# The prologue of a decoder kernel: statistics of all batch elements taken as their tokens land, and transposes placed between keys and values

## The reference

```
x = x + attention(layernorm(x))        # 16 heads of 8, causal, with a relative key term
x = x + cross_attention(layernorm(x), ctx)   # 77 context rows per element, heads normed again
x = x + experts(layernorm(x))          # 8 experts, the best 2 of them, and a shared one
```

## Time and profile before

| | us |
|---|---|
| median of 3 runs | 491.29 (489.8 to 491.65) |
| the profiled execution | 488.51 |
| its span, first to last instruction | 486.7 |
| PE busy in the span | 440.3 (90%) |
| DVE, ACT, POOL busy | 333.7, 265.6, 162.1 |
| first transpose of the prologue on PE | starts at 12.42 |
| first scores of the attention on PE | start at 36.96 |

### The profile page before, as it was taken

The page is one execution under the profiler, slowest core; times in us unless marked ns, Lnnn a source line. Parts: engine busy times, 40 slices in busy tenths (PEclk is TensorE's granted clock), DMA queues, the critical chain, the costliest instruction groups (busy, mean ns, idle before and its releaser), DMA issues.

```text
span 486.7 us, 17235 instructions
## 1 busy us (share of the span) xinstructions
PE 440.3 (90%) x7304; PEld 276.1 (57%) x7304; DVE 333.7 (69%) x668; ACT 265.6 (55%) x811; POOL 162.1 (33%) x95
## 2 busy tenths in 40 slices
PE   0778999999999799999799999998888989999996
PEld 0444655665755555655575675574445435666765
DVE  5555787666977667886847987867677596565633
ACT  2545646666466456555535655545544456554653
POOL 7148384332350963350851432093300000001000
PEclk9999999999999899999889999999989899999999
DMA  8221000000000000000000000000000004404150
GB/s 286 70 73 48 20 9 23 26 18 9 27 25 1 24 18 11 25 24 2 24 4 24 2 5 1 3 4 2 1 1 1 1 1 174 175 23 162 35 195 24
DMA packets 17465, 19.49 MB, mean 40 GB/s; under 512 B 1659, under 2 KB 14575, under 8 KB 17263
## 3 DMA queue, kind: packets, MB, share of 16 engines
q1 hardware_dynamic: 17391, 18.41, 11.2%
HBM read 16.17 MB, written 2.16 MB: 38 GB/s over the span
## 4 chain that ended last, share of the span: by engine, by line
PE 67%; DVE 18%; issue 5%; ACT 5%; DMA 3%; POOL 1%; SPq 0%; DVEq 0%; ACTq 0%; POOLq 0%
PE psT L1489 15%; PE psS L1460 13%; PE psS L1470 8%; PE psOM L1426 7%; PE psT L1859 5%; PE psS L1842 4%; DVE neg_max L1086 2%; DVE x_max L1069 2%; ACT prob L692 2%; PE psOM L1570 2%; PE psS L1689 2%; DMA q_both<-w_scratch 2%; PE psT L1570 2%; DVE pt_even L1050 2%; PE psOM L1716 1%
## 5 line engine op out<-in xcount | busy, mean ns | idle before, releaser
L692 ACT ACTIVATE prob<-psS,neg_max 128x208 f32<-128x208 f32 (+23 forms) x256 | 120.9, 479 | 71.2 <-DVE neg_max L1086 40.1
L475 POOL TENSOR_TENSOR stat<-stat,pack_a_sb 128x4 f32<-128x4 f32 (+2 forms) x16 | 54.7, 3417 | 163.3 <-DVE stat L912 116.9
L1086 DVE TENSOR_REDUCE neg_max<-psS 128x2 f32<-128x672 f32 (+9 forms) x96 | 77.0, 802 | 43.1 <-PE psS L1470 42.3
L1489 PE MATMUL psT<-pack_a_sb,prob 128*128 128x128 f32 (+4 forms) x640 | 95.9, 285 | 6.6 <-DVE pt_even L1050 3.5
L1489 PEld LDWEIGHTS psT<-pack_a_sb,prob 128*128 128x128 f32 (+4 forms) x640 | 65.7, 133 | 45.8 <-issue 27.0
L1460 PE MATMUL psS<-k_v,q_both 64*32 64x336 f32 (+23 forms) x2048 | 88.8, 402 | 3.0 <-ACT prob L692 1.7
L1470 PE MATMUL psS<-rel_shifted,q_both 36*32 36x268 f32 (+16 forms) x2048 | 72.4, 339 | 0.0
L509 POOL TENSOR_TENSOR q_both<-qT,pack_a_sb 128x1024 f32<-128x1024 f32 x16 | 31.7, 1981 | 84.3 <-PE psS L1470 81.9
L1470 PEld LDWEIGHTS psS<-rel_shifted,q_both 36*32 36x32 f32 x2048 | 37.9, 109 | 24.5 <-issue 17.5
L692 ACT ACTIVATION_READ_ACCUMULATOR prob<-psS,neg_max 128x1 f32 x256 | 50.9, 199 | 0.0
L1859 PEld LDWEIGHTS psT<-pack_b_sb,prob 128*128 128x128 f32 x288 | 36.1, 191 | 18.3 <-DVE prob L1332 11.1
(11 more groups left out here) (173 smaller groups left out, 606.7 us busy)
## 6 DMA issues: line engine op xcount, KB each, us to landing
q_rep<-q_scratch SPq DMA_DIRECT2D x128, 32.0 KB
k_v<-w_scratch SPq DMA_DIRECT2D x8, 512.0 KB, 6.6
q_both<-w_scratch SPq DMA_DIRECT2D x8, 512.0 KB, 6.6
pack_b_sb<-pack_b_dram SPq DMA_DIRECT2D x1, 1641.5 KB, 9.7
X<-x_dram SPq DMA_DIRECT2D x4, 256.0 KB, 5.3
q_scratch<-qT SPq DMA_DIRECT2D x4, 256.0 KB, 2.0
out_dram<-X SPq DMA_DIRECT2D x4, 256.0 KB, 2.3
pack_a_sb<-pack_a_dram SPq DMA_DIRECT2D x1, 535.0 KB, 4.4
```

The costliest lines, as they stand in the source:

```text
L475: nc.gpsimd.tensor_tensor(st[:, 5, 0:groups], st[:, 2, 0:groups], ca["root"][0:parts, 0:groups], ALU.pow).then_inc(seeded, 1)
L692: ins = nc.scalar.activation(prob[:, s % 4, half, 0:wide], psS[:, bank + half, at:at + wide], ACT.Exp, bias=neg_max[:, s % 4, half:half + ...
L1086: v.tensor_reduce(neg_max[:, s % 4], psS[:, bank:bank + 2, 0:read_width(*divmod(s, BS))], AX_X, ALU.max, negate=True).then_inc(max_ready, 1)
L1489: ins = nc.tensor.transpose(psT[0:w, k % 2, at:at + T], prob[:, s % 4, half, j * T:j * T + w], ident)
```

## The change

There are five parts.

- SP loads the tokens of elements 2 and 3 ahead of `rel` and the context, right behind those of element 1.
- DVE sums each element when it has landed, into statistics of its own (`stat_first[b]`), and all four sums stand ahead of the first scaling. ACT makes minus the mean, and squares for elements 0, 1, 2 ahead of its first copy, for 3 behind it.
- The subtraction into `xc` is gone. DVE makes `stage` from `X` with four instructions of 128 columns, each `(X + (-mean)) * inverse root` with two scalars per token.
- PE does the transposes of element b+1 between keys and values of element b. ACT's copies go in turn into `xnT` and into a part of `prob`, which has no other use yet.
- POOL clears only `q_rep` and `pt_diag` at first. `V_now`, `x_max` and `spaced` are cleared behind the second `q_rel`, just ahead of the first copy of values into `V_now`.

The diff, cut to its core:

```diff
@@ SP @@
             load_tokens(1)
+            load_tokens(2)
+            load_tokens(3)
             sp.dma_start(rel[:], rel_base).then_inc(rel_base_loaded, 16)
             sp.dma_start(ctx_sb, ctx_in.rearrange("b m d -> m b d")).then_inc(ctx_loaded, 16)
-            load_tokens(2)
-            load_tokens(3)
@@ POOL @@
             nc.gpsimd.memset(q_rep[:], 1.0).then_inc(const_ready, 1)
-            nc.gpsimd.memset(V_now[:], 0.0).then_inc(const_ready, 1)
             nc.gpsimd.memset(pt_diag[:], 0.0).then_inc(const_ready, 1)
-            nc.gpsimd.memset(x_max[:], 0.0).then_inc(x_max_cleared, 1)
-            nc.gpsimd.memset(spaced[:], 0.0).then_inc(x_max_cleared, 1)
...
+                    if first and n == 1:
+                        nc.gpsimd.memset(V_now[:], 0.0).then_inc(const_ready, 1)
+                        nc.gpsimd.memset(x_max[:], 0.0).then_inc(x_max_cleared, 1)
+                        nc.gpsimd.memset(spaced[:], 0.0).then_inc(x_max_cleared, 1)
+                        pool.wait_ge(const_ready, 3)
@@ ACT @@
+                act.wait_ge(ln_sums, b + 1)
+                nc.scalar.activation(st[:, 4, :], st[:, 0, :], ACT.Copy, scale=-1.0 / D).then_inc(ln_means, 1)
...
             squares(0)
-            project(0)
-            project(1)
+            squares(1)
+            squares(2)
+            copy_first(0)
+            squares(3)
+            project_k(0)
+            copy_first(1)
+            project_k(1)
+            copy_first(2)
@@ DVE @@
+            def first_sum(b):
+                dve.wait_ge(x_loaded[b], 16)
+                v.reduce_sum(stat_first[b][:, 0, :], X[:, b * TB:(b + 1) * TB, :], AX_X).then_inc(ln_sums, 1)
...
+            def first_scale(b):
+                dve.wait_ge(ln_var, b + 1)
+                refine(stat_first[b], TB, b)
+                dve.wait_ge(ln_means, b + 1)
+                if b:
+                    dve.wait_ge(psT_ready[1], b + ONE)
+                for t in range(TB):
+                    ins = v.tensor_scalar(stage[:, t, :], X[:, b * TB + t, :], stat_first[b][:, 4, t:t + 1],
+                                          stat_first[b][:, 3, t:t + 1], ALU.add, ALU.mult)
+                ins.then_inc(ln_done, 1)
@@ PE @@
-            project(0)
-            project(1)
+            turn_first(0)
+            project_qk(0)
+            turn_first(1)
+            project_v(0)
+            project_qk(1)
+            turn_first(2)
+            project_v(1)
```

More of the change, by code:

```diff
@@ L123, in build @@
         stage_flat = stage[:].rearrange("p t d -> p (t d)")
+        xn_first = [xnT[:], prob_flat[:, 0:S]]
+        stat_first = [stat[:, :, b * TB:b * TB + TB] for b in range(B)]
         x_pT = [prob_flat[0:M, i * XG * S:(i + 1) * XG * S].rearrange("p (g i) -> p g i", g=XG) for i in range(2)]
@@ L602, in squares, with copy_first, project_k @@
             def squares(b):
+                st = stat_first[b]
+                act.wait_ge(ln_sums, b + 1)
+                nc.scalar.activation(st[:, 4, :], st[:, 0, :], ACT.Copy, scale=-1.0 / D).then_inc(ln_means, 1)
                 act.wait_ge(ln_means, b + 1)
                 for t in range(TB):
[L607 to L608 removed]
+                    ins = nc.scalar.activation(sq[:, t, :], X[:, b * TB + t, :], ACT.Square, bias=st[:, 4, t:t + 1],
+                                               accum_out=st[:, 1, t:t + 1])
                 ins.then_inc(ln_squares, 1)
[L611 removed]
+            def copy_first(b):
                 for half in range(2):
                     act.wait_ge(psT_ready[half], b + 1 + ONE)
[L615 to L617 removed]
+                    if half == 0 and b > 1:
+                        act.wait_ge(psO_ready, b - 1 + ONE)
+                    nc.scalar.activation(xn_first[b % 2][:, half * 256:half * 256 + 256], psT[:, half, 0:256],
                                          ACT.Copy).then_inc(psT_read[half], 1)
[L619 to L620 removed]
+            def project_k(b):
                 act.wait_ge(k_ready, b + 1)
@@ L993, in _ @@
             xc_flat, sq_flat = (a[:].rearrange("p t d -> p (t d)") for a in (xc, sq))
-            c.loop(0, 0, FIRST_LN * B)
[L996 to L1017, removed]
@@ new lines, in _ @@
+            c.loop(0, 0, FIRST_LN * B)
+            first_sum(0)
+            first_sum(1)
+            dve.wait_ge(a_loaded, 16)
+            v.tensor_scalar(rel0[:], ca["rel"][0:HD, :], ca["rel"][0:HD, 0:1], None,
+                            ALU.subtract).then_inc(rel0_ready, 1)
+            first_sum(2)
+            first_variance(0)
+            first_sum(3)
+            first_scale(0)
+            first_variance(1)
+            first_scale(1)
+            project_q(0)
+            first_variance(2)
@@ L1020, in _ @@
+            first_scale(2)
+            project_v(0)
+            project_q(1)
+            first_variance(3)
+            first_scale(3)
+            project_v(1)
+            project_q(2)
+            project_v(2)
+            project_q(3)
+            project_v(3)
             c.done()
```

41 lines of the change are left out of this document (26 added, 15 removed).

## The result

The changed kernel takes 483.66 us (median of 4 runs, 482.54 to 486.85), the kernel before beside it 491.47. The ratio is 0.9873, with a 95% interval of 0.984 to 0.9905, that is 6.2 us; the two medians alone lie 7.8 us apart. Timed a second time (after_again), the same program came to 0.9898 (0.986 to 0.9937), or 5.0 us. The two intervals overlap, and the middle of the two ratios, some 5.6 us, is my best figure for what the change is worth.

A forecast was written before the change was run, and what follows sets the result against it. The prediction saw PE as the bound, with time to fill only in the prologue. A first-scores shift of 5.3 us, 1.2 from the head and 4.1 from the rounds, took 491.29 to 486.0 us, range 483.4 to 489.1.

The forecast's parts named there:

- (a) The head: Prologue before PE's first transposes: they start at 11.25 instead of 12.42, 1.2 us gained.
- the narrow row: Head's scaling: a 64-column instruction at 0.195 us, the basis for taking 0.8 us for four of 128 columns.
- (b) First projections: PE from first transposes to the end of the first keys: 5.3 us as before, ending at 16.55.
- (c) The rounds: PE from the first keys to the first scores: PE-bound if inputs are there, 4.1 us of the shift.
- The list on PE: PE's instructions in order with warm durations, from the first keys to the last values: 13.7 us, ending at 30.25.
- The margin that I gave DVE: DVE's chain for elements 2 and 3: 3.5 us against a PE round of 3.5, started early, margin about 1 us.
- The signs: Checks in the profile: first transposes near 11.3, first scores near 31.7, attention's end (about 334) moving by the same amount.
- The clearings moved: POOL's three clearings, 3.3 us, now beside the attention: cost 0, at most 3.3 us if they held DVE.
- The late load: Head not shorter: element 2 lands near 9.3, transposes at 12.9, shift 3.6, 487.7 us; chance 0.12.
- The better case: Prologue: loads and scaling at low bounds, rounds without a gap, shift 6.5 to 7.5, 484.3 us; chance 0.12.
- A gain given back in the attention: Moved clearings hold DVE's copies for 3.3 us in the attention: shift 2.0, 489.3 us; chance 0.09.
- The slower case: After the prologue: a denser prologue lowers PE's later clock, 493.9 us at a loss of 0.024; chance 0.05.

The follow-up runs named there:

- centre_scale: The changed kernel with centring and scaling as two instructions of 512 columns again, instead of four of 128; 0.9909 of the kernel before.
- warm_pe: The changed kernel with three extra matmuls on TensorE ahead of the first transposes; 0.9852 of the kernel before.
- reordered: all_three with ACT's first copy ahead of element 2's squares and DVE's variances ahead of the query and value biases; 481.12 us, 0.982 of the kernel before.
- clear_first: The changed kernel with all five clearings at the head of GpSimd's program again; 0.9913 of the kernel before.
- before_clear: The kernel before with only three of the clearings moved behind the second q_rel; 0.9958 of the kernel before.
- all_three: The changed kernel with first variance behind first sum, first scores not waiting for the last values' bias, two matmuls ahead of the first transposes; 0.9862.
- sums_back: The changed kernel with sum and squares of elements 1 to 3 in their rounds again, each ahead of its variance; 1.0012 of the kernel before.

## Why the prediction was right

**The mechanism.** I had said that the shift of the first scores is the gain, that it has a small part from the head and a large one from rounds that become bound by TensorE. It was 6.5 us, 1.0 and 5.5, against 5.3, 1.2 and 4.1; in the second profile 5.6.

**(a) The head, 1.0 instead of 1.2.** The path was the one I had: up to the scaling it ran as forecast to within 0.1 us (sum of element 2 at 7.59 instead of 7.65, scaling from 10.25 instead of 10.3). The mean on ACT cost 0.20 instead of 0.3, which changed nothing, since the variance waited for the third sum and not for the squares. The term that was off is the four scalings: they cost 1.11 instead of 0.8, near the upper bound; the narrow row was the wrong neighbour, the 0.29 of a 128-column instruction the nearer one. The Trainium skill's advice in "VectorE: DVE Perf Modes" ("The TRN2 errata"), that short instructions lose by a fixed part, agrees with the rows in direction (1.11 us for four of 128 columns, 0.69 for one tensor_tensor of 512), and its table's estimate of 0.5 us does not; yet the split beats two instructions of 512 columns, as centre_scale shows.

**(b) First projections, as said.** 16.82 - 11.46 = 5.36 against 5.3.

**(c) The rounds.** The list on PE was summed to 13.7, and measured 12.5 from 16.82 to 29.3. The term that was mis-sized is the instruction's own duration taken for its share of the engine. In the chain the three rounds of transposes take 1.4 instead of 2.0, the queries 1.06, 0.90 and 0.86 instead of 1.10 each, the context's transposes 0.27 instead of 0.4. The rows suggest why: where the input is there, the weight load starts ahead of its matmul (26.40 and 26.50 for the last queries), and where PE has waited, the two start 0.03 us apart (20.71 and 20.74 before). That and the 0.3 allowed for hand-overs make up the difference, 1.5 us.

The margin that I gave DVE was wrong the other way. From the scaling of element 2 to that of element 3 it took 4.23 us, not 3.5:

```profile
17.76 1.12 DVE L1033 TENSOR_SCALAR stage<-X,stat 128x128 f32<-128x128 f32 x4
18.79 0.68 DVE L1007 TENSOR_TENSOR k_v<-psOM,pack_a_sb 128x512 f32<-128x512 f32 x1
...
21.99 1.12 DVE L1033 TENSOR_SCALAR stage<-X,stat 128x128 f32<-128x128 f32 x4
```

My list left out the bias of the values, which stands in DVE's program between that scaling and the bias of the queries: 0.60 us. The scaling is most of the rest (1.03 us to the next instruction instead of 0.8). So `stage` came 2.3, 1.1 and 0.2 us ahead of the transposes of elements 1, 2 and 3, and the 1 us that I had counted on for each was used up at the last. That PE was never held is luck: its slow start had put it late, and warm_pe, without the slow start, shows DVE's round. In reordered the variances stand ahead of the biases, and no matmul waits for `stage`.

**Sum.** 5.3 us predicted; by the ratios 6.2 and 5.0 us were measured, by the medians 7.8 and 6.3. The mechanism was right; that the number is this near is in part luck, since the head and DVE's list were too short and PE's list too long.

**The signs.** The first transposes came at 11.46 (11.3 said), the first scores at 30.47 (31.7), element 2 in time for 7.59, no wait of PE for its input stands between 17 and 29 us, and the clearings begin at 34.6. The attention's end was to move by as much as the first scores. In the first profile it did not: its last matmul is at 328.4 instead of 333.4, 5.0 us for 6.5. In the second it did, 327.8, 5.6 us for 5.6. The difference is the longer stretch at the lower clock.

**The clearings moved: nothing, as said.** clear_first and before_clear show the head's gain with its sign both ways, and rows beside the attention show no price. The rule of the Trainium skill's page "SBUF — State Buffer" on the shared port pair agrees in three kernels: 3.10, 1.51 and 0.87 us for instructions on four columns, each ending with a clearing. My sentence on it was wider than the page, which names copies, casts and tensor_scalar and leaves out reductions; the rows agree with the page, since the sums took their 0.69 us beside a clearing.

**The rivals.** The late load did not occur, though the loads' order is worth 1.0 to 1.2 us of the head. The better case was the nearer one in the moments (6.5 shift) and in the median. A gain given back in the attention is not shown: in the second profile the attention takes 294.7 us from its first scores to the cross attention, 294.6 before. The slower case asked whether a denser prologue lowers the later clock, and this stays open. The mean clock was 0.979 and 0.981 in the two profiles against 0.982; over the timed executions it was 0.977 in the second timing against 0.980 for the kernel before beside it, with single ones from 0.965 to 0.986. Behind the prologue the stretches at 0.50 sum to 20.4 us in eight of the twelve profiles with the changed prologue or most of it, and to 17.0 in both profiles with the old one; two of those are too few to tell.

## What to carry to other kernels

When a chain of small steps goes through four engines once per element, take the steps that depend on the input alone out of the round; only then does it pay to reorder what is left on the bound engine. Sum an engine's round from every instruction that stands in it, also those that serve another element: the bias of the values was the 0.6 us that my sum had missed. After such an edit look at every in-order program that the moved result passes, not only the one edited: the first copy, behind the squares of a later element, held PE for 2.0 and 2.3 us instead of 0.5 here. And read a prologue's edit by moments of more than one profile, since the time of a run carries the clock's spread on top, and the moments of one execution that of the slow start.

## What the hardware showed that I had not expected

- Instructions of the vector engine on 128x4 elements wait for a clearing on GpSimd to end, up to 3 us, while its reductions and its copies from PSUM beside the same clearings do not (0.69 and 0.68).
- The slow pace of TensorE at the start does not show in the granted clock, which reads 1.00 there; a later fall does, with 0.50. The durations are the same in both, 1.91 us for the keys of element 0 in the changed kernel's first profile at 1.00 and in all_three at 0.50, so both are the lower of the two levels, 1.2 of 2.4 GHz. In the prologue the pace fell again behind waits of 2.3 us (all_three) and 3.1 us (sums_back), and not in the wait but up to a microsecond after work had begun again; behind waits of 0.6 to 1.5 it did not (kernel before: 1.49 us ahead of 25.34, and the queries behind it in 1.10). The slow start ended about a microsecond apart in two executions of one program.
- The mean granted clock hides this. A mean of 0.98 was 1.00 nearly everywhere and 0.50 in four stretches, 17 or 20 us in all. What came before the other three stretches I did not follow.
- The mean granted clock of one program ranged from 0.965 to 0.986 between executions. The changed kernel's spans were 480.8 at 0.981 and 485.1 at 0.972, in the second timing 482.1 at 0.986 and 487.5 at 0.965, so 0.01 is worth some 3 to 5 us, up to nearly the whole change.
- The load of element 1, 256 KB issued at 1.77, landed between 6.4 and 7.4 us in these profiles, with the same queue in front of it.
